# The last scan's chunks are turned by one GpSimd copy in place of two half copies

## The chip, the cores and the metric

The kernel runs on one core of a Trainium2 chip. The metric is the device time of one launch in microseconds (us), here the median of three runs. The engines of a core run side by side, each through its own instruction list, and meet at semaphores: TensorE (PE), VectorE (DVE), ScalarE (ACT), GpSimd (POOL) and SyncE (SP). A DMA is issued from the list of SP, ACT or POOL.

## The reference

```python
# L2: sums and gradients over the same edges; the gradient is what is used
def get_H(xx):
    z = xx @ W_fc.T
    e = sigmoid(concat([z[src], z[dst]]) @ W_attn.T)
    w = exp(e - segment_max(e, dst)[dst])
    h = segment_sum(w / segment_sum(w, dst)[dst] * z[src], dst)
    h1 = segment_sum((h @ W_encK.T + b_encK)[src], dst)
    K = _mlp3(h1, K_w0, ...)                      # per node
    ue = (h @ W_p1.T + b_p1)[src] + (h @ W_p2.T + b_p2)[dst]
    U = _mlp3(ue, U_w0, ...)                      # per edge
    E_new = segment_sum(K[src] * U, dst)
    return sum(E_new)
dHdx = grad(get_H)(x)
return dHdx @ J.T - dHdx @ D.T

# the whole: four layers over the same 106250 edges and 6250 nodes
x = x + L0(relu(layernorm(x)))    # graph attention
x = x + L1(relu(layernorm(x)))    # five graph convolutions with norms
x = x + L2(relu(layernorm(x)))    # the gradient above
x = x + L3(relu(layernorm(x)))    # mean over neighbours, then a product
```

In the backward pass of the third layer the gradient with respect to `ue` is one row of 64 numbers per edge, and it has to be summed twice, once over the edges with the same source and once over the edges with the same destination. The edge list is sorted by destination, so the sum over equal destinations is a running sum along the list that starts anew where the destination changes. This second sum is the stage that the change touches. The program calls it "dsum".

## The kernel before

**Layout.** 106496 edge places (106250 edges and padding) lie as 128 partitions by `J` = 832 places. A chunk is `CJ` = 32 places of each partition with 64 features, that is 128x2048 numbers of float32 (1024 KB); there are `2 * IT` = 26 chunks. In DRAM the tensor `xd` holds the 64 features of an edge side by side, and so does the buffer `DX` that a chunk is read into. A scan runs along the edges of one feature, so the chunk is first turned into feature order in a buffer `DM`: the 32 places of feature 0, then those of feature 1, and so on. `DX`, `DM`, the mask `DMASK` (in PSUM) and the output buffer `DOUT` exist twice each and alternate, chunk k uses number k % 2.

**One chunk k, in the order of its data:**

- ACT issues the read of the rows into `DX` (`rows_act`, line 2250), on its own DMA queue.
- ACT writes the mask, 0 where the destination changes (`before_scan_act`, lines 2255 and 2257).
- DVE turns features 0 to 31 (`half_turned`, line 2039) and ACT turns features 32 to 63 (line 2259). Both read `DX` in steps of 64 numbers and write `DM` without gaps. ACT's half signals `prepared`.
- DVE adds the carried sum to each feature's first place (line 624), scans twice 1024 numbers (line 629) and copies the 64 last sums into `carry` for the next chunk (line 631). This copy signals `scanned`.
- ACT turns the sums back into edge order in `DOUT` (line 2265, `dsum_out`), waits for that copy with a drain (line 2266) and issues the write to the DRAM tensor `runs` (line 2267).

**What sets the order.** Everything is written out by hand. On DVE the list per chunk is: wait for `prepared`, signal `free` (the row buffer may be filled again), the four scan instructions, then the half turn of chunk k+1. On ACT it is: issue the read of chunk k+2, output copy and write of chunk k, then mask and half turn of chunk k+2. The turns of chunk k+2 write the buffer `DM` that the output copy of chunk k reads, so they wait for `dsum_out`.

**Around the stage.** Ahead of it POOL scatters the last rows into `xd` (line 488) and DVE ends another sum. Behind it, when all 26 writes have landed, DVE signals `carried`; PE, POOL and DVE then join runs that cross partitions, and POOL fetches the 50 blocks of node sums (`ends_pool`, line 485). From its last scatter into `xd` to `carried` POOL has nothing to do.

The functions below are the five engine programs and what they call; the lines named above are the ones to look for.

Of the kernel before, what the change touches and what calls it, by code (L numbers as in the profile page):

```python
# [18 lines left out]
CJ = 32  # L19
IT = J // CJ // 2  # L20
# [58 lines left out]
def build(nc, x_in, src_in, dst_in, src_t_in, w_in, weights_in, vectors_in, out):  # L79
    ctx = ExitStack()  # L80
    with ctx:
# [8 lines left out]
        S = Semaphores()  # L90

        def sb(name, shape, dt=F32):
            return ctx.enter_context(nc.sbuf_tensor(name, shape, dt))
# [39 lines left out]
        firsts = [sb(f"first_same{b}", [P, 1]) for b in range(2)]  # L133
# [25 lines left out]
        OD, OS = Order("d", 0), Order("s", 1)  # L159
# [7 lines left out]
        def region(at, n):  # L167
            assert at + n <= SIZE
            return arena[:, at:at + n]
# [5 lines left out]
        def rows(buf, f, n=CJ):  # L175
            return buf[:, 0:n * f].rearrange("p (j f) -> p j f", f=f)
# [10 lines left out]
        def by_edge(t):  # L187
            return t[0:EP, :].rearrange("(p j) f -> p j f", j=J)
# [10 lines left out]
        def by_feature(buf, f, at=0):  # L199
            return buf[:, at * CJ:(at + f) * CJ].rearrange("p (f j) -> p f j", f=f)  # L200
# [141 lines left out]
        DX = [region(37092 + b * 2048, 2048) for b in range(2)]  # L342
        DM, DOUT = [region(41188, 2048), region(34148, 2048)], [region(19200, 2048), region(32100, 2048)]
# [19 lines left out]
        FREE = {n: TURN[n] * (IT + 1) for n in TURN}  # L363
        SCANNED = {n: TURN[n] * (2 * IT + 1) for n in TURN}
        PREPARED = {n: TURN[n] * 2 * IT for n in TURN}
        LOADS = {"scores": 16, "umlp": 32, "dsum": 16}
        LOADED = {"scores": 0, "umlp": 16 * IT, "dsum": 48 * IT}
# [6 lines left out]

        PRODUCTS = [("kvq", 32, 384), ("Wo", 32, 128), ("A", 32, 512), ("D_T", 32, 128), ("L3", 64, 64)]
        ORDINAL = {n: k for k, (n, _, _) in enumerate(PRODUCTS)}
        DEPTH = {n: d for n, d, _ in PRODUCTS}
        WIDTH = {n: w for n, _, w in PRODUCTS}

        def batches(name):  # L380
# [4 lines left out]
        for name, _, _ in PRODUCTS:  # L385
            FIRST[name] = total
            total += len(batches(name))
# [96 lines left out]
        def fetch(pool, dst, table, index):  # L484
            return pool.indirect_dma_start(dst, None, table, bass.IndirectOffsetOnAxis(ap=index, axis=0))  # L485

        def put(pool, table, index, source):
            return pool.indirect_dma_start(table, bass.IndirectOffsetOnAxis(ap=index, axis=0), source, None)  # L488
# [131 lines left out]
        def scan(dve, mask, buf, f, kept, at=0, to=None, wide=32, goes_on=None):  # L620

            to = buf if to is None else to
            first = by_feature(buf, f, at)[:, :, 0]
            dve.scalar_tensor_tensor(first, kept[:, at:at + f], m0[:] if goes_on is None else goes_on, first, ALU.mult, ALU.add)
            dve.drain()
            for a in range(0, f, wide):
                n = min(f - a, wide)
                piece = slice((at + a) * CJ, (at + a + n) * CJ)
                dve.tensor_tensor_scan(to[:, piece], mask[:, 0:n * CJ], buf[:, piece], 0.0, ALU.mult, ALU.add)  # L629
            dve.drain()  # L630
            return dve.tensor_copy(kept[:, at:at + f], by_feature(to, f, at)[:, :, CJ - 1])
# [34 lines left out]
        def ends_pool(pool, name, o, f, to):  # L666
            n = TURN[name]
            pool.wait_ge(S["carried"], n + 1)
            pool.wait_ge(S["order_joined"], o.n + 1)
            fetch(pool, joined[:, 0:f], R[f], o.join[:]).then_inc(S["join_read"], 16)  # L670
            pool.wait_ge(S["join"], n + 1)
            put(pool, R[f], o.join[:], joined[:, 0:f]).then_inc(S["joined"], 16)
            pool.wait_ge(S["joined"], 16 * (n + 1))
            for t in range(NT):
                fetch(pool, to[:, t * f:(t + 1) * f], R[f], o.end[:, t:t + 1]).then_inc(S["ends"], 16)
# [936 lines left out]
        def _(dve):  # L1612
# [346 lines left out]
            for k in range(2 * IT):  # L1959
                b = k % 2  # L1960
# [70 lines left out]

            begin(dve, carry[:, 0:64], *DMASK)

            def half_turned(k):

                dve.wait_ge(S[f"loaded{k % 2}"], LOADED["dsum"] + LOADS["dsum"] * (k // 2 + 1))
                if k >= 2:
                    dve.wait_ge(S["dsum_out"], k - 1)
                dve.tensor_copy(by_feature(DM[k % 2], 32), rows(DX[k % 2], 64).rearrange("p j f -> p f j")[:, 0:32, :])

            half_turned(0)
            for k in range(2 * IT):
                b = k % 2
                dve.wait_ge(S["prepared"], PREPARED["dsum"] + k + 1)
                dve.drain()
                dve.sem_inc(S[f"free{b}"], 1)
                scan(dve, DMASK[b], DM[b], 64, carry, goes_on=firsts[b][:]).then_inc(S["scanned"], 1)
                if k + 1 < 2 * IT:
                    half_turned(k + 1)
                dve.drain()  # L2050
            carried_dve(dve, "dsum")
            ends_dve(dve, "dsum", 64, bank[3])
# [98 lines left out]
        def _(act):  # L2151
# [77 lines left out]
            for k in range(2 * IT):  # L2229
                b = k % 2  # L2230
# [15 lines left out]

            def rows_act(k):
                b = k % 2
                act.wait_ge(S[f"free{b}"], FREE["dsum"] + k // 2 + 1)
                act.dma_start(rows(DX[b], 64), by_edge(XD)[:, step(k), :]).then_inc(S[f"loaded{b}"], 16)  # L2250

            def before_scan_act(k):
                b = k % 2
                act.wait_ge(S["scanned"], SCANNED["dsum"] + max(1, k))
                act.copy(by_feature(DMASK[b], 32)[:, :, 1:CJ],
                         OD.same[:, k * CJ + 1:(k + 1) * CJ].unsqueeze(1).broadcast_to([P, 32, CJ - 1]))
                act.copy(firsts[b][:], OD.same[:, k * CJ:k * CJ + 1])
                act.wait_ge(S[f"loaded{b}"], LOADED["dsum"] + LOADS["dsum"] * (k // 2 + 1))
                act.copy(by_feature(DM[b], 32, 32), rows(DX[b], 64).rearrange("p j f -> p f j")[:, 32:64, :]).then_inc(S["prepared"], 1)

            def after_scan_act(k):
                b = k % 2
# [6 lines left out]
            for b in range(STAGES):  # L2269
                act.wait_ge(S[f"given{b}"], 256 * len(range(b, 52, STAGES)))  # L2270
            rows_act(0)
            rows_act(1)
            before_scan_act(0)
            before_scan_act(1)
            for k in range(2 * IT):
                if k + 2 < 2 * IT:
                    rows_act(k + 2)
                after_scan_act(k)
                if k + 2 < 2 * IT:
                    before_scan_act(k + 2)  # L2280
# [173 lines left out]
        def _(pool):  # L2454
# [66 lines left out]
            def load(c):  # L2521
                if c >= STAGES:
                    pool.wait_ge(S[f"given{c % STAGES}"], 256 * (c // STAGES))
                pool.wait_ge(S[f"d_kept{c // 2 % 2}"], CREDIT + 16 * (c // 4 + 1))
                pool.dma_start(staged(c % STAGES), edges16(DE, c)).then_inc(S[f"to_give{c % STAGES}"], 16)
# [3 lines left out]
            for c in range(52):  # L2529
                pool.wait_ge(S[f"to_give{c % STAGES}"], 16 * (c // STAGES + 1))  # L2530
                for j in range(16):
                    if j == 8 and c + 2 < 52:
                        load(c + 2)
                    put(pool, XD, at_d[:, 16 * c + j:16 * c + j + 1],
                        GS[c % STAGES][:, j * 64:(j + 1) * 64]).then_inc(S[f"given{c % STAGES}"], 16)
                if c == HD_AT:
                    ends_pool(pool, "umlp", OS, P, HD)
                if c == GK_AT:
                    pool.wait_ge(S["tables_kept"], 16 * 5)
                    fetch(pool, GK[:, NS * 32:NT * 32], TB["gk"], alias_i[:]).then_inc(S["alias_whole"], 16)  # L2540
            ends_pool(pool, "dsum", OD, 64, DD)
            pool.wait_ge(S["tables_kept"], 16 * 6)
            await_made(pool, "shift_made")
# [193 lines left out]
```

## Time and profile before

| | us |
|---|---|
| median of 3 runs | 9476.88 |
| lowest and highest run | 9472.27, 9494.99 |
| the profiled execution's own time | 9485.84 |
| its span in the profile | 9484.0 |
| the stage of the change in it, first read issued to last write issued | 8170.78 to 8360.00 |
| busy over the whole span: PE, DVE, ACT, POOL | 4877.8, 4601.9, 2819.5, 5429.2 |

The engines' busy time over the whole kernel says little of one stage. The stage is read by the timeline of its stretch, by the groups of instructions in it, and by the chain that ended last, each cut to that stretch. Times inside the program are counted from the span's start.

### The profile page before, as it was taken

What the parts mean: (1) busy time and instruction counts of PE and PEld (TensorE: products, weight loads), DVE (VectorE), ACT (ScalarE), POOL (GpSimd) and SP (SyncE); (2) the same over time, 40 slices, a digit from 0 to 9 for tenths busy, and PEclk for the clock granted to TensorE, in tenths of its full rate; (3) what the DMA queues carried; (4) which work ended last, traced back from release to release, by engine and by line L of the source; (5) the groups of instructions that cost most, each with busy time, mean ns of one, the idle gap of its engine ahead of it and who ended that gap; (6) DMA issues with size and microseconds to landing.
All of it is one profiled execution on the core that took longest, in us unless ns stands there. A gap on an engine that the chain in (4) does not pass through costs nothing.

```text
span 9484.0 us, 77287 instructions
## 1 busy us (share of the span) xinstructions
PE 4877.8 (51%) x27914; PEld 2625.5 (28%) x27914; DVE 4601.9 (49%) x6100; ACT 2819.5 (30%) x2192; POOL 5429.2 (57%) x5420
## 2 busy tenths in 40 slices
PE   1000007999257777775577665344440035038976
PEld 0000006888112232331222222244430023032333
DVE  5677776777000000000298960388885510428870
ACT  0111110000000000000198950266667600429850
POOL 3777767777777777777520017688877777320000
PEclk5555555555578989887698975676765568559986
DMA  8666536443398989999799999455559948538767
GB/s 186 215 222 220 205 83 137 154 153 141 155 415 356 415 359 411 365 362 415 279 283 268 288 204 379 144 202 206 203 191 370 342 147 336 187 85 282 263 222 291
DMA packets 1203136, 2404.24 MB, mean 254 GB/s; under 512 B 566439, under 2 KB 818794, under 8 KB 1171354
## 3 DMA queue, kind: packets, MB, share of 16 engines
q1 hardware_dynamic: 996986, 2076.35, 61.7%
q0 software_dynamic: 187136, 170.29, 6.9%
q10 hardware_dynamic: 18720, 153.79, 4.2%
q8 instruction: 171, 2.80, 0.1%
q14 instruction: 123, 1.01, 0.0%
HBM read 1606.44 MB, written 711.62 MB: 244 GB/s over the span
## 4 chain that ended last, share of the span: by engine, by line
POOL 37%; DMA 25%; issue 12%; PE 11%; ACT 7%; ACTq 4%; DVE 3%; SPq 1%; DVEq 0%; POOLq 0%
POOL arena L485 18%; DMA arena<-cells_w 14%; POOL xd L488 9%; POOL cells_w L488 9%; DMA arena<-cells_c 8%; PE ps L698 6%; ACT arena L1030 3%; ACTq L1029 3%; ACT arena L1028 2%; PE ps L787 2%; PE ps L879 1%; ACTq L2266 1%; PE ps L1053 1%; PE ps L1161 1%; DMA arena<-hot 1%
## 5 line engine op out<-in xcount | busy, mean ns | idle before, releaser
L698 PE MATMUL ps<-arena 128*64 128x458 f32 (+2 forms) x7252 | 1349.0, 655 | 701.2 <-DMA arena<-cells_w 699.7
L485 POOL DMA_INDIRECT arena<-t_a,arena x832 | 945.9, 1137 | 1094.9 <-DMA t_a<-arena 841.7
L1053 PE MATMUL ps<-arena 128*33 128x400 f32 x6336 | 1165.1, 522 | 310.1 <-DVE arena L1048 302.4
L488 POOL DMA_INDIRECT sorted<-arena x832 | 839.7, 1009 | 288.9 <-issue 288.9
L716 DVE COPY carry<-ps 64x128 f32<-64x128 f32 (+1 forms) x5 | 1.5, 295 | 2048.2 <-PE ps L698 2048.2
L488 POOL DMA_INDIRECT xd<-arena x832 | 832.7, 1001 | 256.4 <-issue 253.2
L488 POOL DMA_INDIRECT cells_c<-arena x832 | 810.5, 974 | 292.6 <-issue 292.6
L488 POOL DMA_INDIRECT cells_w<-arena x832 | 813.0, 977 | 276.8 <-issue 276.8
L485 POOL DMA_INDIRECT arena<-t_kv,idx x832 | 816.9, 982 | 258.7 <-issue 253.3
L698 PEld LDWEIGHTS ps<-arena 128*64 128x64 f32 (+1 forms) x7252 | 426.2, 147 | 1621.1 <-issue 856.4
L1053 PEld LDWEIGHTS ps<-arena 128*33 128x33 f32 x6336 | 366.6, 115 | 1106.4 <-issue 652.8
L1555 ACT ACTIVATE norm_cols<-norm_cols 128x1 f32<-128x1 f32 x5 | 1.0, 203 | 2235.0 <-DVE norm_cols L1537 2235.0
L1042 DVE TENSOR_TENSOR arena<-arena 128x1600 f32<-128x1600 f32 x328 | 597.3, 1821 | 96.0 <-ACT arena L1032 42.9
L1270 PE MATMUL ps<-arena 128*128 128x50 bf16 x832 | 72.4, 219 | 1055.3 <-DVE arena L1258 1055.3
L1048 DVE SCALAR_TENSOR_TENSOR arena<-arena 128x1600 f32<-128x1600 f32 x328 | 598.8, 1826 | 25.9
L629 DVE TENSOR_TENSOR_SCAN arena<-ps,arena 128x512 f32<-128x512 f32 (+2 forms) x494 | 591.4, 1263 | 7.6
L1030 ACT ACTIVATE arena<-arena,half 128x1600 f32<-128x1600 f32 x328 | 534.5, 1630 | 24.5 <-issue 2.4
L1369 PE MATMUL ps<-arena,packT 128*128 128x50 f32 x1664 | 434.8, 412 | 0.0
L1369 PEld LDWEIGHTS ps<-arena,packT 128*128 128x128 f32 x1664 | 434.7, 336 | 0.0
L879 PE MATMUL ps<-arena 128*64 128x400 f16 x1568 | 280.9, 508 | 248.3 <-DMA arena<-cells_c 227.6
L1032 ACT ACTIVATE arena<-arena 128x1600 f32<-128x1600 f32 x246 | 374.2, 1521 | 0.0
L801 PE MATMUL ps<-ident,arena 128*64 128x128 f32 x300 | 20.7, 308 | 652.4 <-DVEq L209 651.7
(536 smaller groups left out, 9097.3 us busy)
## 6 DMA issues: line engine op xcount, KB each, us to landing
arena<-cells_w SPq DMA_DIRECT2D x245, 3200.0 KB
arena<-cells_c SPq DMA_DIRECT2D x294, 800.0 KB, 5.3
arena<-cells_turned SPq DMA_DIRECT2D x200, 800.0 KB, 8.5
cells_w<-arena SPq DMA_DIRECT2D x49, 3200.0 KB, 20.4
weighed_cells<-arena SPq DMA_DIRECT2D x68, 1600.0 KB, 14.4
arena<-weighed_cells SPq DMA_DIRECT2D x68, 1600.0 KB, 7.2
cells_c<-arena SPq DMA_DIRECT2D x50, 1600.0 KB, 5.8
cells_turned<-arena SPq DMA_DIRECT2D x100, 800.0 KB, 5.4
```

What stands on the lines that cost most here:

```text
L485: return pool.indirect_dma_start(dst, None, table, bass.IndirectOffsetOnAxis(ap=index, axis=0))
L488: return pool.indirect_dma_start(table, bass.IndirectOffsetOnAxis(ap=index, axis=0), source, None)
L629: dve.tensor_tensor_scan(to[:, piece], mask[:, 0:n * CJ], buf[:, piece], 0.0, ALU.mult, ALU.add)
L698: mm = pe.matmul(bank[base + k][g * f:(g + 1) * f, 0:m], rows_of, tile[:, g * width + at:g * width + at + m], start=first, stop=last, skip ...
L879: mm = pe.matmul(bank[(4 if i == 0 else 0) + c][64 * g:64 * g + 64, 0:400], pieces, moving[:, a:a + 400], start=first, stop=last, skip_gro ...
L1029: act.drain()
L1030: last = act.activation(expo[b], tanh[b], ACT.Exp, scale=0.5, bias=half[:])
L1032: last = act.activation(tanh[b], tanh[b], ACT.Square)
L1042: last = dve.tensor_tensor(expo[b], expo[b], piece_of(counts_of(name, p), h), ALU.mult)
L1048: dve.scalar_tensor_tensor(tanh[b], tanh[b], -1.0, expo[b], ALU.add, ALU.mult).then_inc(S["weighed"], 1)
L1053: last = pe.matmul(bank[4 * h + c][64 * kind:64 * kind + 33, 0:400], own[:, t, :], moving[:, 400 * c:400 * c + 400], start=t == 0, stop=do ...
L1369: pe.matmul(to[:, 0:NT], packT[k % 2][:, i * P:(i + 1) * P], snap[k % 2][:, i * NT:(i + 1) * NT], start=True, stop=True, skip_group_check= ...
```

## The change

POOL gets a loop over the 26 chunks ahead of `ends_pool`. For each it waits for the chunk's rows and, from the third on, for the output copy of chunk k-2, then turns all 64 features with one copy of 128x2048 and signals `dsum_turned`. DVE's and ACT's half turns go. DVE's scan of chunk k waits for `prepared` (now signalled by ACT's copy of the first mask column) and for `dsum_turned`. DVE no longer signals `free` in the loop: ACT's read of chunk k+2 waits for `dsum_turned` of chunk k.

```diff
--- before.py
+++ after.py
@@ -2031,22 +2031,11 @@
 
             begin(dve, carry[:, 0:64], *DMASK)
 
-            def half_turned(k):
-
-                dve.wait_ge(S[f"loaded{k % 2}"], LOADED["dsum"] + LOADS["dsum"] * (k // 2 + 1))
-                if k >= 2:
-                    dve.wait_ge(S["dsum_out"], k - 1)
-                dve.tensor_copy(by_feature(DM[k % 2], 32), rows(DX[k % 2], 64).rearrange("p j f -> p f j")[:, 0:32, :])
-
-            half_turned(0)
             for k in range(2 * IT):
                 b = k % 2
                 dve.wait_ge(S["prepared"], PREPARED["dsum"] + k + 1)
-                dve.drain()
-                dve.sem_inc(S[f"free{b}"], 1)
+                dve.wait_ge(S["dsum_turned"], k + 1)
                 scan(dve, DMASK[b], DM[b], 64, carry, goes_on=firsts[b][:]).then_inc(S["scanned"], 1)
-                if k + 1 < 2 * IT:
-                    half_turned(k + 1)
                 dve.drain()
             carried_dve(dve, "dsum")
             ends_dve(dve, "dsum", 64, bank[3])
@@ -2246,7 +2235,10 @@
 
             def rows_act(k):
                 b = k % 2
-                act.wait_ge(S[f"free{b}"], FREE["dsum"] + k // 2 + 1)
+                if k < 2:
+                    act.wait_ge(S[f"free{b}"], FREE["dsum"] + 1)
+                else:
+                    act.wait_ge(S["dsum_turned"], k - 1)
                 act.dma_start(rows(DX[b], 64), by_edge(XD)[:, step(k), :]).then_inc(S[f"loaded{b}"], 16)
 
             def before_scan_act(k):
@@ -2254,9 +2246,7 @@
                 act.wait_ge(S["scanned"], SCANNED["dsum"] + max(1, k))
                 act.copy(by_feature(DMASK[b], 32)[:, :, 1:CJ],
                          OD.same[:, k * CJ + 1:(k + 1) * CJ].unsqueeze(1).broadcast_to([P, 32, CJ - 1]))
-                act.copy(firsts[b][:], OD.same[:, k * CJ:k * CJ + 1])
-                act.wait_ge(S[f"loaded{b}"], LOADED["dsum"] + LOADS["dsum"] * (k // 2 + 1))
-                act.copy(by_feature(DM[b], 32, 32), rows(DX[b], 64).rearrange("p j f -> p f j")[:, 32:64, :]).then_inc(S["prepared"], 1)
+                act.copy(firsts[b][:], OD.same[:, k * CJ:k * CJ + 1]).then_inc(S["prepared"], 1)
 
             def after_scan_act(k):
                 b = k % 2
@@ -2538,6 +2528,11 @@
                 if c == GK_AT:
                     pool.wait_ge(S["tables_kept"], 16 * 5)
                     fetch(pool, GK[:, NS * 32:NT * 32], TB["gk"], alias_i[:]).then_inc(S["alias_whole"], 16)
+            for k in range(2 * IT):
+                pool.wait_ge(S[f"loaded{k % 2}"], LOADED["dsum"] + LOADS["dsum"] * (k // 2 + 1))
+                if k >= 2:
+                    pool.wait_ge(S["dsum_out"], k - 1)
+                pool.tensor_copy(by_feature(DM[k % 2], 64), rows(DX[k % 2], 64).rearrange("p j f -> p f j")).then_inc(S["dsum_turned"], 1)
             ends_pool(pool, "dsum", OD, 64, DD)
             pool.wait_ge(S["tables_kept"], 16 * 6)
             await_made(pool, "shift_made")

```

DVE's list of the stage, before: one scan and the half turn of the next chunk (the arena is the big SBUF buffer that `DX`, `DM` and `DOUT` are parts of).

```order
3356 L2039 COPY arena<-arena 128x1024 [waits loaded0]
3357 L624 SCALAR_TENSOR_TENSOR arena<-carry,first_same,arena 128x64 [waits prepared]
3358 L629 SCALAR_TENSOR_TENSOR arena<-ps,arena 128x1024 x2
3359 L631 COPY carry<-arena 128x64
3360 L2039 COPY arena<-arena 128x1024 [waits loaded1]
```

DVE's list of the stage, of the changed kernel:

```order
3356 L624 SCALAR_TENSOR_TENSOR arena<-carry,first_same,arena 128x64 [waits dsum_turned,prepared]
3357 L629 SCALAR_TENSOR_TENSOR arena<-ps,arena 128x1024 x2
3358 L631 COPY carry<-arena 128x64
3359 L624 SCALAR_TENSOR_TENSOR arena<-carry,first_same,arena 128x64 [waits dsum_turned,prepared]
3360 L629 SCALAR_TENSOR_TENSOR arena<-ps,arena 128x1024 x2
```

The copy of 128x1024 between two scans is gone, and the first instruction of a scan waits for POOL beside ACT.

ACT's list, before, from the read of chunk 2 to the read of chunk 3:

```order
1258 L2250 DMA arena<-xd 128x2048 [waits free0]
1259 L2265 COPY arena<-arena 128x2048 [waits stored0,scanned]
1260 L2267 DMA runs<-arena 128x2048
1261 L2255 CAST ps<-same_d 128x32x31 [waits scanned]
1262 L2257 CAST first_same<-same_d 128x1
1263 L2259 COPY arena<-arena 128x1024 [waits loaded0]
1264 L2250 DMA arena<-xd 128x2048 [waits free1]
```

ACT's list of the changed kernel at the same place (L2242 is the read, L2255 the output copy, L2257 the write, L2247 the mask, L2249 its first column):

```order
1256 L2242 DMA arena<-xd 128x2048 [waits dsum_turned]
1257 L2255 COPY arena<-arena 128x2048 [waits stored0,scanned]
1258 L2257 DMA runs<-arena 128x2048
1259 L2247 CAST ps<-same_d 128x32x31 [waits scanned]
1260 L2249 CAST first_same<-same_d 128x1
1261 L2242 DMA arena<-xd 128x2048 [waits dsum_turned]
```

ACT's half turn is gone, and the read waits for POOL's copy in place of DVE's signal.

POOL's list of the changed kernel behind the last scatter into `xd`; before, the row behind `L488 ... x15` was the fetch `joined<-runs,join_d`:

```order
821 L488 DMA xd<-arena 106496x64 x15
822 L2535 COPY arena<-arena 128x2048 [waits loaded0]
823 L2535 COPY arena<-arena 128x2048 [waits loaded1]
824 L2535 COPY arena<-arena 128x2048 [waits dsum_out,loaded0]
825 L2535 COPY arena<-arena 128x2048 [waits dsum_out,loaded1]
...
848 L485 DMA joined<-runs,join_d 128x64 [waits order_joined,carried]
```

26 copies stand ahead of the join fetch, two of them with no wait for an output copy.

## Rows read from the trace of the kernel before

**Rows 1.** The chain that ended last, shares by line, of 8140 to 8380 us.

```profile
by line: ACTq L2266 35.2%; ACT arena L2259 18.4%; issue 10.3%; POOL xd L488 9.3%; ACT ps L2255 4.6%; POOL arena L485 3.6%; ACTq L2267 3.3%; ACT arena L2265 3.1%; DMA arena<-xd 2.0%; DVE arena L629 1.9%; DVEq L630 1.8%; ACT first_same L2257 
```

**Rows 2.** Timeline of one steady step: start us, us, engine, line, operation, idle before.

```profile
8195.39 0.22 DVE L631 COPY carry<-arena 128x64 f32<-128x64 f32 x1
...
8196.98 3.70 ACT L2265 COPY arena<-arena 128x2048 f32<-128x2048 f32 x1
8197.22 0.35 DVE L624 SCALAR_TENSOR_TENSOR arena<-carry,first_same,arena 128x64 f32<-128x64 f32 x1 [0.66 <-ACT arena L2259]
8197.64 4.47 DVE L629 TENSOR_TENSOR_SCAN arena<-ps,arena 128x1024 f32<-128x1024 f32 x2
8200.75 0.33 ACTq L2267 DMA_DIRECT2D runs<-arena  x1
8201.11 0.99 ACT L2255 CAST ps<-same_d 128x992 f32<-128x992 bf16 x1 [0.43 <-issue]
...
8202.13 1.93 ACT L2259 COPY arena<-arena 128x1024 f32<-128x1024 f32 x1
...
8203.96 3.69 ACT L2265 COPY arena<-arena 128x2048 f32<-128x2048 f32 x1
```

**Rows 3.** Groups of instructions, 8170 to 8364 us: count | busy us, mean ns | idle before.

```profile
L2265 ACT COPY arena<-arena 128x2048 f32<-128x2048 f32 x26 | 96.1, 3696 | 4.3 <-DVE carry L631 4.3
L2259 ACT COPY arena<-arena 128x1024 f32<-128x1024 f32 x26 | 50.1, 1928 | 3.0 <-DMA arena<-xd 3.0
L2039 DVE COPY arena<-arena 128x1024 f32<-128x1024 f32 x26 | 26.8, 1032 | 113.7 <-DMA arena<-xd 113.7
L2255 ACT CAST ps<-same_d 128x992 f32<-128x992 bf16 x26 | 25.7, 989 | 631.4 <-DMA xd<-arena 620.7 <-issue 10.7
```

**Rows 4.** Timeline of the first two chunks.

```profile
8175.72 1.93 ACT L2259 COPY arena<-arena 128x1024 f32<-128x1024 f32 x1 [2.97 <-DMA arena<-xd]
...
8177.80 0.33 DVE L624 SCALAR_TENSOR_TENSOR arena<-carry,first_same,arena 128x64 f32<-128x64 f32 x1 [1.05 <-ACT arena L2259]
...
8182.77 0.21 DVE L631 COPY carry<-arena 128x64 f32<-128x64 f32 x1
...
8183.02 3.71 ACT L2265 COPY arena<-arena 128x2048 f32<-128x2048 f32 x1 [2.52 <-DVE carry L631]
8184.13 0.34 DVE L624 SCALAR_TENSOR_TENSOR arena<-carry,first_same,arena 128x64 f32<-128x64 f32 x1 [0.20 <-issue]
...
8189.08 0.22 DVE L631 COPY carry<-arena 128x64 f32<-128x64 f32 x1
```

**Rows 5.** Timeline of the last chunk.

```profile
8356.02 0.21 DVE L631 COPY carry<-arena 128x64 f32<-128x64 f32 x1
8356.27 3.66 ACT L2265 COPY arena<-arena 128x2048 f32<-128x2048 f32 x1 [1.77 <-DVE carry L631]
```

**Rows 6.** Timeline of an earlier stage, where DVE and POOL work at once.

```profile
7026.57 2.11 POOL L488 DMA_INDIRECT xd<-arena  x1 [0.31 <-issue]
7026.58 1.98 DVE L1982 COPY arena<-arena 128x2048 f32<-128x2048 f32 x1
...
7028.99 0.97 POOL L488 DMA_INDIRECT xd<-arena  x1 [0.30 <-issue]
7029.18 2.34 DVE L629 TENSOR_TENSOR_SCAN arena<-ps,arena 128x512 f32<-128x512 f32 x2
```

**Rows 7.** Line 631's copies, ns min/median/max: 5960 to 7720, then 8170 to 8364.

```profile
L631 DVE COPY carry<-arena x26: 266/324/440, 6135.9 to 7103.6; 128x128 f32<-128x128 f32 x26
...
L631 DVE COPY carry<-arena x26: 213/215/222, 8182.8 to 8356.0; 128x64 f32<-128x64 f32 x26
```

**Rows 8.** Groups of instructions on POOL: the widest and the smallest IOTA.

```profile
L2460 POOL IOTA arena<- 128x832 int32 x1 | 0.8, 811 | 0.0
...
L2458 POOL IOTA arena<- 128x1 int32 x1 | 0.1, 128 | 0.0
```

**Rows 9.** Busy us (count) per engine in 21 steady steps, PE clock, DMA share, GB/s.

```profile
8196.00:8342.00 146.00, 0.00 (x0) 0.00 (x0) 124.97 (x104) 136.62 (x84) 0.00 (x0) 0.50 0.83 299
```

## The prediction

> **What bounds the kernel now.** I read the chain of waits of the stretch first, then one step in the timeline, then the groups. In the chain, ACT's lines hold the last scan: 35.2% under the drain behind the output copy (line 2266), 18.4% under ACT's half turn (2259), 4.6% under the mask [rows 1]. DVE's scan has under 2% of it. The timeline of a step says the same: ACT goes from one output copy to the next in 8203.96 - 8196.98 = 6.98 us, and that time is its own work from end to end: 3.70 for the output copy, 4.13 from that copy's start to the mask's start (the copy, the drain and the issue of the write), 0.99 for the mask, the first column, 1.93 for its half turn. DVE waits 0.66 us for line 2259 before its scan [rows 2]. Of 146 steady microseconds ACT is busy 136.62, DVE 124.97, POOL 0; the DMA engines are at 0.83 of their time, the PE clock is 0.50 and PE has no work [rows 9]. So today the period is ACT's list, some 6.93 us: line 631 ends at 8182.98 for chunk 0 and at 8356.23 for chunk 25, 173.25 us for 25 steps [rows 4, 5].
>
> **What is removed.** ACT loses 26 half turns of 1.928 us, DVE 26 of 1.032 us, 77 us of busy time in all [rows 3]. Without them ACT needs 6.98 - 1.93 = 5.05 us a chunk. DVE needs from line 631's start to the next one's start 8189.08 - 8182.77 = 6.31 us where it hardly waits [rows 4], 5.28 without its half turn. If nothing took the place of the turns, DVE would bound the stage at about 5.3 us a chunk.
>
> **What is added.** One POOL copy of 128x2048 per chunk; call its time X. No row of the trace shows a compute copy on POOL, so I bound it. From below: POOL's widest IOTA writes 832 numbers in 811 ns and the smallest takes 128, so it writes one number in 0.82 ns and 2048 in 0.128 + 1.68 = 1.81 us, if reading cost nothing [rows 8]. But the read goes in steps of 256 bytes. ACT, with the same buffer and the same steps, has 1.928 us for 1024 and 3.696 for 2048 in its other strided copy [rows 3], or 1.73 ns a number. If the memory sets that pace for POOL too, X is 0.13 + 3.54 = 3.67 us. From above: if POOL's loop reads and then writes, the two paces add, and X is 0.13 + 3.54 + 1.68 = 5.35 us. The nearest rows are twice ACT's half turn, 3.86 us, and the output copy, 3.70; POOL's own fixed 0.13 goes on top, and I take X = 4.0 us, with 3.67 and 5.35 as likely ends and 1.81 as the far one.
>
> The Trainium skill speaks against this change: "GPSIMD Engine Reference", section "Performance pitfalls for Q7 kernels", has about 2.9 cycles for each element read with a step over 8 bytes, 1.9 for a smaller one. At its 1.2 GHz an estimate from that page is 2048 x 2.9 / 1.2 = 4.95 us, and the sum below would be +55 us with it; no run here shows such a copy yet.
>
> **Where X lies on the path.** The turn of chunk k+2 writes the buffer that the output copy of chunk k reads, so it starts only when that copy is done, as both half turns did. The loop through the buffer is: line 631 of chunk k ends, 0.04 us to ACT, 3.70 us output copy, a wake of about 0.15 (from 8177.65 to 8177.80 for ACT to DVE), X, 0.15 again, then the scan of chunk k+2 from line 624 to the end of 631, 8189.30 - 8184.13 = 5.17 us [rows 3, 4]. That loop covers two chunks, so the period is at least (9.21 + X) / 2. For X = 4.0 this is 6.6 us, a little under today's 6.93. Before, the same loop had 1.93 in the place of X and had slack, which is why ACT's list and not this loop was the bound.
>
> **A second meeting, which I think decides.** When POOL turns chunk k+2, DVE scans chunk k+1, and at the scan's end comes line 631, a copy from SBUF to SBUF. Rows 6 show such a copy and POOL excluding each other: POOL's DMA instruction started beside line 1982's copy and lasted to 7028.68, the copy ending at 7028.56, while beside the scan of line 629 (mask in PSUM) a POOL instruction took its usual 0.97 [rows 6]. Rows 7 show a cost in the other direction: line 631 takes 266 to 440 ns where POOL issues DMAs all the time, and 213 to 222 in the last scan, where POOL has nothing to do [rows 7]. So I expect line 631 to wait until POOL's copy is done. Line 624 has two SBUF inputs, but it stands before the next turn has started and should not meet one.
>
> The Trainium skill's page "SBUF — State Buffer", section "Who interferes with whom", calls this an exclusive lock on a shared port pair, held for a whole instruction. Its first half, DVE holding POOL up, is in the trace with the 2.11 us of rows 6; that a POOL copy holds DVE up for its whole length, no row here shows.
>
> With that wait, `scanned` of chunk k+1 comes after the turn of chunk k+2, and ACT's next output copy after that. The loop is now one chunk long: 0.04 + 3.70 + 0.15 + X + 0.12 + 0.21 = 4.22 + X, where 0.12 is the release seen in rows 6 and 0.21 is line 631 [rows 4, 6]. For X = 4.0 the period is 8.22 us. The turn starts 3.9 us after line 631's end and the scan wants its line 631 after 5.2, so the two meet for every X over 1.3.
>
> **The sum.** Chunks 0 to 24 are 24 periods apart, and the last step has no turn beside it: 0.18 + 5.17 = 5.35 us. That is 24 x 8.22 + 5.35 = 202.6, against 173.25: +29.4. The first scan waits for a whole turn, X, in place of ACT's 1.93 [rows 4]: +2.1. Behind the stage all stands as before; POOL's copies are all ahead of the join fetch, for which it waited anyhow. The reads of rows are issued one output copy earlier than they are used and have a period of time to land, so they stay hidden at 8.22 us; the DMA engines, at 0.83 before, are less loaded. In total +31.5 us, and in general 25 X - 68.5. The profiled execution has 9485.84 us, 9 above the median of 9476.88; the difference does not depend on it, so I add it to each: 9517 for a like execution, 9508.4 for the median. A measurement of this kernel can tell about 0.3%, 28.4 us, from no change; with the wait that is X over 3.88.
>
> **The rivals.**
>
> - *No wait at line 631.* POOL's copy and DVE's small one pass each other. For it: the only DVE copies seen beside POOL's work are delayed by 0.2 us at most, not by whole instructions [rows 7]. Against it: line 1982 did hold POOL. The period is (9.21 + X) / 2, the sum 24 times that + 5.35 - 173.25 + X - 1.93 = 13 X - 59.3. For 4.0 it is -7 us, 9469.6; for 3.67 -12; for 5.35 +10. All within 0.3%.
> - *A slow copy and the wait.* If the copy's read and write add, X = 5.35, the period is 9.57 and the sum +65, 9542. It decides how far the slower side goes.
> - *Faster: a copy at the pace of the IOTA, and no wait.* X = 1.81 gives a period of 5.5, or 5.8 if the DMAs' 0.83 x 6.97 us of work per chunk cannot shrink [rows 2, 9]: -29 to -36 us, 9441 to 9448. It needs X under 2.4 and no wait. With the wait a copy of 1.81 gives -23 us, 9454. Against it: ACT cannot read this pattern at such a pace [rows 3].
> - *The change does nothing for the busy engines.* ACT's and DVE's 77 us of busy time go in any case; in the first and second case they turn into idle time.
>
> **How the numbers follow.** The wait at line 631 gets 0.70. X over 3.88 gets 0.70 too: the nearest rows give 3.67 to 3.86 as floors, and a loop in software only adds. X under 3 gets 0.10. Both together give 0.49 for slower by over 0.3%, and 0.01 goes on top for something unseen: 0.50. Forecast and slow copy share this, 0.35 near the forecast and 0.15 far above. Faster by over 0.3% needs no wait and a fast copy: 0.03, with 0.02 for the unseen, 0.05. The rest, 0.45, is within 0.3%: no wait with any copy of 2.4 or more (about 0.28), and the wait with a copy under 3.88 (about 0.17). The range goes from the rival without the wait at X = 3.67, 9465, to the slow copy, 9542, with a microsecond or two on each side.
>
> **What would show it.** Right: POOL copies of about 4 us each starting as ACT's output copy ends; line 631 lasting or starting late until a POOL copy ends, its mean far over 215 ns or a gap ahead of it; ACT idle some 3 us per chunk ahead of the output copy; chunks 8.2 us apart. Wrong in the size: the same picture with another X, the period following it one for one. Wrong in the mechanism: line 631 still at 215 ns behind its scan while POOL's copy runs, and DVE waiting ahead of line 624 for POOL, the period following X by half. It would be wrong altogether if the reads of rows landed late, which would show as POOL waiting for `xd`.

## The result

| | median us | runs |
|---|---|---|
| kernel before | 9483.82 | 19 |
| changed kernel | 9502.77 (9487.11 to 9511.15) | 19 |
| ratio | 1.0018, 95% interval 1.0011 to 1.0025 | |

The change costs about 17 us, between 10 and 24: slower, but by less than the 0.3% that the prediction set as its bound. On another occasion the unedited changed kernel gave 1.0021 (1.0012 to 1.0030). The forecast was 9508.4 us in a range of 9463 to 9544. The mechanism that it named is in the trace; of the 31.5 us forecast, the trace has 19.9 and the medians 19.0.

Three groups of the changed kernel's last scan, of 8170 to 8390 us, answer to [rows 3] (count | busy us, mean ns | idle before). Line numbers have moved: L2255 is ACT's output copy (before L2265), L2535 the new copy on POOL. L631 is the copy of 64 sums behind each scan, with 5.6 us in all before.

```profile
L2255 ACT COPY arena<-arena 128x2048 f32<-128x2048 f32 x26 | 96.6, 3716 | 72.4 <-DVE carry L631 72.4
L2535 POOL COPY arena<-arena 128x2048 f32<-128x2048 f32 x26 | 95.0, 3656 | 106.1 <-ACT arena L2255 96.1 <-DMA arena<-xd 10.0
L631 DVE COPY carry<-arena 128x64 f32<-128x64 f32 x26 | 60.3, 2320 | 1.9
```

POOL's copy takes 3.66 us. The small copy takes 2.32 us in the mean, 0.22 before [rows 7]. ACT waits for it 72.4 us in all, where it had waited 4.3 us before [rows 3]. The timeline shows one step, and answers to [rows 2]:

```profile
8197.32 3.65 POOL L2535 COPY arena<-arena 128x2048 f32<-128x2048 f32 x1 [8.85 <-ACT arena L2255]
8197.62 0.99 ACT L2247 CAST ps<-same_d 128x992 f32<-128x992 bf16 x1 [0.43 <-issue]
...
8198.58 2.46 DVE L631 COPY carry<-arena 128x64 f32<-128x64 f32 x1
8201.07 3.73 ACT L2255 COPY arena<-arena 128x2048 f32<-128x2048 f32 x1 [2.34 <-DVE carry L631]
8201.20 0.36 DVE L624 SCALAR_TENSOR_TENSOR arena<-carry,first_same,arena 128x64 f32<-128x64 f32 x1 [0.16 <-POOL arena L2535]
8201.63 4.47 DVE L629 TENSOR_TENSOR_SCAN arena<-ps,arena 128x1024 f32<-128x1024 f32 x2
...
8204.93 3.65 POOL L2535 COPY arena<-arena 128x2048 f32<-128x2048 f32 x1 [3.96 <-ACT arena L2255]
...
8206.18 2.47 DVE L631 COPY carry<-arena 128x64 f32<-128x64 f32 x1
8208.68 3.72 ACT L2255 COPY arena<-arena 128x2048 f32<-128x2048 f32 x1 [2.34 <-DVE carry L631]
```

POOL's copy ends at 8200.97, line 631 at 8201.04, ACT starts at 8201.07. The scans themselves (line 629, 4.47 us) are untouched, with POOL's copy beside them. The period is 7.61 us: 0.03 to ACT, 3.73 the output copy, 0.13 to POOL, 3.65 the turn, 0.07 to the end of line 631. In the chain that ended last, DVE's lines have taken the place of ACT's of [rows 1]:

```profile
by line: DVE carry L631 23.2%; DVE arena L629 22.9%; DVEq L630 21.8%; POOL xd L488 10.1%; issue 6.0%; DVE arena L624 4.8%; DMA arena<-xd 1.8%; DMA runs<-arena 1.5%; POOL arena L485 1.5%; ACT arena L2255 1.4%; POOL arena L2535 1.4%; DMA join
```

The start of the stage holds one thing more (timeline; the read of the rows was issued at 8176.50):

```profile
8181.23 7.23 POOL L2535 COPY arena<-arena 128x2048 f32<-128x2048 f32 x2 [5.94 <-DMA arena<-xd]
8184.91 0.33 ACTq L2242 DMA_DIRECT2D arena<-xd  x1
8184.99 3.60 DVE L624 SCALAR_TENSOR_TENSOR arena<-carry,first_same,arena 128x64 f32<-128x64 f32 x1 [116.88 <-POOL arena L2535]
8188.67 4.47 DVE L629 TENSOR_TENSOR_SCAN arena<-ps,arena 128x1024 f32<-128x1024 f32 x2
8193.22 0.21 DVE L631 COPY carry<-arena 128x64 f32<-128x64 f32 x1
```

POOL turns the first two chunks back to back. Line 624, an operation with two inputs in SBUF, takes 3.60 us in place of 0.33 [rows 4], to the end of the second turn.

### The profile page after: what moved, and what is told of

Its sections match the earlier page's. It is cut to its first block, busy times and chain, and to the rows that moved or that the text cites. A ratio compares the mean times of both kernels' runs of the same rounds, so it can differ in the third digit from the quotient of the medians.

```text
span 9506.9 us, 77261 instructions
## 1 busy us (share of the span) xinstructions
PE 4893.7 (51%) x27914; PEld 2636.2 (28%) x27914; DVE 4641.0 (49%) x6074; ACT 2774.4 (29%) x2166; POOL 5536.2 (58%) x5446
## 4 chain that ended last, share of the span: by engine, by line
POOL 37%; DMA 25%; issue 12%; PE 11%; ACT 6%; DVE 4%; ACTq 3%; DVEq 1%; SPq 1%; POOLq 0%
POOL arena L485 18%; DMA arena<-cells_w 14%; POOL xd L488 9%; POOL cells_w L488 9%; DMA arena<-cells_c 8%; PE ps L698 5%; ACT arena L1030 4%; ACTq L1029 3%; ACT arena L1028 2%; PE ps L787 2%; DMA arena<-hot 1%; PE ps L879 1%; PE ps L1161 1%; PE ps L1053 1%; DVE carry L631 1%
## 5 line engine op out<-in xcount | busy, mean ns | idle before, releaser
L488 POOL DMA_INDIRECT sorted<-arena x832 | 844.2, 1015 | 289.6 <-issue 289.6
L488 POOL DMA_INDIRECT xd<-arena x832 | 835.2, 1004 | 256.5 <-issue 253.5
L488 POOL DMA_INDIRECT cells_c<-arena x832 | 813.2, 977 | 293.1 <-issue 293.1
L488 POOL DMA_INDIRECT cells_w<-arena x832 | 815.9, 981 | 275.9 <-issue 275.9
L1270 PE MATMUL ps<-arena 128*128 128x50 bf16 x832 | 72.4, 219 | 1057.0 <-DVE arena L1258 1057.0
```

## The experiments

The theory: a copy on POOL and a DVE operation that uses a second way into SBUF (a copy from SBUF to SBUF, or an operation with two inputs there) exclude each other; so line 631 waits, and through it ACT. The rivals: the loop through the two buffers `DM` holds the stage up; POOL's copy is simply too long, whatever it meets; the reads of the rows come late.

The stage is compared by the time from the start of the first line 631 to the start of the last, 25 steps: 173.2 us before (8182.8 to 8356.0, [rows 7]), 188.4 in the changed kernel (8193.2 to 8381.6).

The first four kernels shared a chip on which the earlier stages took about 4000 us longer (the kernel before 13606.67 us, with 13234.67 to 13935.94 between runs). Of them only the last scan's rows are used. One of the four is the kernel before with its carry moved, and it has before's own period there (173.3 us for 25 steps), which shows that these rows can be used.

**Carry in PSUM, twice.** The 64 carried sums move out of SBUF. Line 631 then writes PSUM, line 624 has one SBUF input.

```diff
-            begin(dve, carry[:, 0:64], *DMASK)
+            dcarry = bank[7][:, 0:64]
+            begin(dve, dcarry, *DMASK)
...
-                scan(dve, DMASK[b], DM[b], 64, carry, goes_on=firsts[b][:]).then_inc(S["scanned"], 1)
+                scan(dve, DMASK[b], DM[b], 64, dcarry, goes_on=firsts[b][:]).then_inc(S["scanned"], 1)
...
+            dve.tensor_copy(carry[:, 0:64], dcarry)
+            dve.drain()
             carried_dve(dve, "dsum")
```

> The changed kernel with the 64 carried sums kept in PSUM during the last scan (copied to SBUF once at its end), so that the small copy behind each scan (line 631) writes PSUM and the first operation of a scan (line 624) has one SBUF tensor input. If the small copy waits because it and GpSimd's copy exclude each other, it takes about 0.2 us again, ScalarE's output copy follows it at once, and the period falls from 7.61 us to the two-chunk loop, (9.2 + 3.66) / 2 = 6.4 us: 24 x 1.2 = 28 us less than the changed kernel, and the first scan does not wait for the second turn, 3 us more. Against the kernel before that is about -13 us, ratio 0.9987. If DVE is held up by something else (a semaphore, GpSimd slowing all of VectorE), the period stays at 7.6.

> The changed kernel with the carried sums in PSUM, once more, because its first run shared a chip whose times varied by 700 us. Its last scan was 168.2 us long there (first small copy to last), against 188 of the changed kernel and 173 of the kernel before, with GpSimd waiting for the rows in most chunks. By that the kernel should be about 20 us under the changed kernel plus 3 us for the first scan, and 3 to 5 us under the kernel before: ratio 0.9994 to 0.9999.

Measured: in both runs line 631 takes 0.27 to 0.30 us with POOL's copy around it. The timeline of the second run (L2538 is POOL's copy, L2258 the output copy, L2245 the read of rows, L2260 the write):

```profile
8252.79 3.67 POOL L2538 COPY arena<-arena 128x2048 f32<-128x2048 f32 x1 [2.31 <-DMA arena<-xd]
8252.92 0.99 ACT L2250 CAST ps<-same_d 128x992 f32<-128x992 bf16 x1 [0.43 <-issue]
8252.96 0.40 ACTq L2245 DMA_DIRECT2D arena<-xd  x1
8253.84 0.19 ACT L2252 CAST first_same<-same_d 128x1 f32<-128x1 bf16 x1
8255.53 0.27 DVE L631 COPY ps<-arena 128x64 f32<-128x64 f32 x1
8255.83 3.68 ACT L2258 COPY arena<-arena 128x2048 f32<-128x2048 f32 x1 [1.81 <-DVE ps L631]
...
8259.88 3.70 POOL L2538 COPY arena<-arena 128x2048 f32<-128x2048 f32 x1 [3.42 <-DMA arena<-xd]
```

The group of POOL's copies in the same run:

```profile
L2538 POOL COPY arena<-arena 128x2048 f32<-128x2048 f32 x26 | 95.6, 3681 | 81.5 <-DMA arena<-xd 71.1 <-ACT arena L2258 10.4
```

Line 631 runs inside POOL's copy (8252.79 to 8256.46) and ACT follows at once. The 25 steps take 168.2 and 167.4 us, some 20 less than in the changed kernel, and the kernel is back at the time before: 0.9996 (0.9987 to 1.0005). Line 624 had 328 ns in the mean, with no long one among the 26, so its wait in the first chunk is gone as well. This settles the main question: POOL's copy is as long as before (3.68 us), so its length alone was not the cause. It also narrows what waits. In its first chunk line 624, now with one of its two tensor inputs in PSUM, took 0.33 us inside POOL's second turn, and the scans, with their mask in PSUM, took their usual time. Both read and write SBUF as well, so reading and writing SBUF once beside POOL's copy is not by itself enough for a wait. What passed had one tensor operand in PSUM, what waited had none; which of the small copy's two ends in SBUF held it, no run separates.

It misses the 6.4 us period expected: it is 6.7, and POOL waits for its rows 71.1 us in all (in the timeline the read was issued at 8252.96, and the copy of those rows started at 8259.88). ACT issued that read behind its output copy and write, though POOL's copy of 8246.81 had freed the row buffer at 8250.48. That the reads behind ACT's list are the next bound is what these waits suggest; no run changed them alone in this kernel.

**Carry in PSUM in the kernel before**, as the control.

> Control: the kernel before with the carried sums in PSUM in the same way. GpSimd has nothing to do in that stage and ScalarE's list sets the period, so both theories expect no difference: period 6.93 to 6.98 us, the kernel's time within 3 us of the kernel before.

Measured: line 631 from 12417.0 to 12590.3 us, 173.3 for 25 steps. No difference, as both theories said; moving the carry gains nothing by itself, only against POOL's copy.

**Three buffers in feature order.**

```diff
-        DM, DOUT = [region(41188, 2048), region(34148, 2048)], ...
+        DM, DOUT = [region(41188, 2048), region(34148, 2048), region(12800, 2048)], ...
...
-                if k >= 2:
-                    pool.wait_ge(S["dsum_out"], k - 1)
+                if k == 2:
+                    pool.wait_ge(S["scanned"], SCANNED["dsum"] + 1)
+                if k >= 3:
+                    pool.wait_ge(S["dsum_out"], k - 2)
```

with `DM[k % 3]` in POOL's copy, the scan and the output copy.

> The changed kernel with three buffers in feature order in place of two, so that the turn of chunk k+2 waits for the output copy of chunk k-1 and not of chunk k. The carry stays in SBUF. If the buffer were what holds the changed kernel up, the period would fall to about 5.4 to 5.8 us. If the wait of the small copy is what holds it up, a turn still lies beside the end of some scan: the small copy still waits, and the period stays between 6.6 us (the turn started by the landing of its rows) and 7.6 us (started by the output copy).

Measured: 11945.0 to 12121.7 us, 176.7 for 25 steps, 7.07 a step; between the two bounds of the exclusion theory. Two neighbouring steps say more than the mean (L2537 is POOL's copy):

```profile
12003.45 3.65 POOL L2537 COPY arena<-arena 128x2048 f32<-128x2048 f32 x1 [2.22 <-DMA arena<-xd]
12006.28 0.89 DVE L631 COPY carry<-arena 128x64 f32<-128x64 f32 x1
...
12008.35 3.79 POOL L2537 COPY arena<-arena 128x2048 f32<-128x2048 f32 x1 [1.24 <-DMA arena<-xd]
...
12012.30 0.21 DVE L631 COPY carry<-arena 128x64 f32<-128x64 f32 x1
```

The first POOL copy ends at 12007.10, and line 631, begun at 12006.28, at 12007.17. The second ends at 12012.14, and line 631, begun 0.16 later, takes its 0.21. The longest small copy of this run starts just behind a POOL copy and lasts as long as it does:

```profile
12038.66 3.63 POOL L2537 COPY arena<-arena 128x2048 f32<-128x2048 f32 x1 [5.11 <-DMA arena<-xd]
12038.74 3.62 DVE L631 COPY carry<-arena 128x64 f32<-128x64 f32 x1
```

All 26 follow this: 17 overlap a POOL copy and end 0.06 to 0.14 us behind it, the other 9 take 0.21 to 0.22.

**Three buffers, the rows read by SyncE.** In the run above the start of a turn was mostly set by its rows. Here SP issues the reads, as soon as a row buffer is free.

```diff
+            for k in range(2 * IT):
+                b = k % 2
+                if k < 2:
+                    sp.wait_ge(S[f"free{b}"], FREE["dsum"] + 1)
+                else:
+                    sp.wait_ge(S["dsum_turned"], k - 1)
+                sp.dma_start(rows(DX[b], 64), by_edge(XD)[:, k * CJ:(k + 1) * CJ, :]).then_inc(S[f"loaded{b}"], 16)
```

in SP's list behind `back_sp(sp, range(2))` and the waits for `given`, and no `rows_act` in ACT's.

> The changed kernel with three buffers in feature order and the reads of the rows issued by SyncE as soon as their row buffer is free, where ScalarE's list delayed them in the run with three buffers. The carry stays in SBUF. Nothing but the output copy of chunk k-1 then holds a turn back, and it ends 3.9 us after a small copy, in the middle of the next scan: by the exclusion theory the small copy of that scan waits and the period is again near 4.0 + 3.66 = 7.6 us. If the buffers or the late reads were the cause, the period falls to about 5.8 us, what the DMA engines need for 2 MB a chunk.

Measured: ratio 1.0019 (1.0009 to 1.0028), line 631 from 8198.4 to 8383.6 us, 185.2 for 25 steps, with 2210 ns in the mean:

```profile
L2525 POOL COPY arena<-arena 128x2048 f32<-128x2048 f32 x26 | 94.7, 3643 | 98.1 <-ACT arena L2247 90.7 <-DMA arena<-xd 7.4
L631 DVE COPY carry<-arena 128x64 f32<-128x64 f32 x26 | 57.5, 2210 | 1.9
```

With more buffers and early rows the step is back at 7.4 us in the mean, against 7.5 in the changed kernel: nearly all of POOL's idle time ends with an output copy (90.7 us), in the middle of the next scan. The loop through the buffers is excluded as the cause, and so are the rows.

**The same with the carry in PSUM.**

> The same with the carried sums in PSUM, so that no VectorE operation of the loop excludes GpSimd's copy. ScalarE needs 5.05 us a chunk, VectorE 5.4, GpSimd 3.7, the DMA engines 5.7 to 5.8 (0.83 of 6.97 us before). Period about 5.8 us, 145 us for 25 steps in place of 173 before and 188 in the changed kernel: 26 us less than the kernel before, ratio 0.997.

Measured: ratio 0.9980 (0.9971 to 0.9989), 9458.85 us against 9478.74 for the kernel before and 9499.40 for the changed kernel on the same chip. It beats both, the kernel before by 0.2%. It differs from the run above in the carry alone. 25 steps take 152.6 us (8176.6 to 8329.2), 6.1 each; one of the shorter ones in the timeline (L2528 is POOL's copy, L2250 the output copy, L2252 the write):

```profile
8262.64 0.27 DVE L631 COPY ps<-arena 128x64 f32<-128x64 f32 x1
8262.70 0.19 ACT L2244 CAST first_same<-same_d 128x1 f32<-128x1 bf16 x1
8262.95 3.79 ACT L2250 COPY arena<-arena 128x2048 f32<-128x2048 f32 x1
8263.07 0.35 DVE L624 SCALAR_TENSOR_TENSOR arena<-ps,first_same,arena 128x64 f32<-128x64 f32 x1 [0.16 <-ACT first_same L2244]
8263.50 4.47 DVE L629 TENSOR_TENSOR_SCAN arena<-ps,arena 128x1024 f32<-128x1024 f32 x2
8266.80 0.33 ACTq L2252 DMA_DIRECT2D runs<-arena  x1
8266.87 3.80 POOL L2528 COPY arena<-arena 128x2048 f32<-128x2048 f32 x1 [1.66 <-ACT arena L2250]
8267.17 0.99 ACT L2242 CAST ps<-same_d 128x992 f32<-128x992 bf16 x1 [0.43 <-issue]
8268.04 0.27 DVE L631 COPY ps<-arena 128x64 f32<-128x64 f32 x1
```

5.4 us lie between these two small copies. Other steps take longer, for a reason that the waits name (engine and line, for whom: us in total, times, longest):

```profile
POOL arena L2528 <- ACT arena L2250: 38.4, 16, 4.8
POOL arena L2528 <- DMA arena<-xd: 23.7, 9, 6.0
DVE arena L624 <- ACT first_same L2244: 21.6, 24, 4.1
ACT arena L2250 <- DMA runs<-arena: 19.7, 8, 4.2
```

ACT waits 19.7 us for its earlier writes to `runs` to land, which it did nowhere before. Over 8200 to 8325 us the DMA engines are busier than in the kernel before (same columns as [rows 9]; before first, then this run):

```profile
8200.00:8325.00 125.00, 0.00 (x0) 0.00 (x0) 106.72 (x90) 116.92 (x73) 0.00 (x0) 0.50 0.83 299
8200.00:8325.00 125.00, 0.00 (x0) 0.00 (x0) 101.99 (x81) 97.42 (x61) 72.68 (x20) 0.50 0.89 329
```

That the transfers are the next bound fits, but no run here took bytes away to show it. The expectation of 5.8 us was 0.3 too low.

**A copy that turns nothing.** POOL copies the same 128x2048 numbers, reading them without gaps; the turning is left out.

```diff
-                pool.tensor_copy(by_feature(DM[k % 2], 64), rows(DX[k % 2], 64).rearrange("p j f -> p f j"))...
+                pool.tensor_copy(by_feature(DM[k % 2], 64), by_feature(DX[k % 2], 64))...
```

> The changed kernel with GpSimd's copy of the same 128x2048 numbers reading without gaps, so nothing is turned (the turning is left out). If the step of 256 bytes sets the copy's pace, it takes about 1.8 to 2.1 us in place of 3.66, and since the period follows it one for one it comes to about 5.9 us: 24 x 1.7 = 41 us less than the changed kernel. If the copy's loop on GpSimd sets the pace, it stays near 3.7 us and the time stays.

Measured (group of POOL's copies):

```profile
L2535 POOL COPY arena<-arena 128x2048 f32<-128x2048 f32 x26 | 49.2, 1893 | 299.8 <-DMA arena<-xd 270.1 <-ACT arena L2255 29.7
```

1.893 us against 3.656: the step of 256 bytes costs POOL 1.76 us, nearly half of its copy. The 25 steps took 157.2 us (12430.6 to 12587.8), 6.3 each and not the 5.9 expected, and POOL waited for rows ahead of 19 of 26 copies; as above, that points to the reads behind ACT's list. Line 631 still waited, 0.57 us in the mean, where the shorter copy reached the end of a scan.

**Half of the change.** GpSimd takes ACT's features 32 to 63, DVE keeps features 0 to 31.

```diff
-                act.copy(by_feature(DM[b], 32, 32), rows(DX[b], 64).rearrange("p j f -> p f j")[:, 32:64, :]).then_inc(S["prepared"], 1)
...
+                pool.tensor_copy(by_feature(DM[b], 32, 32), rows(DX[b], 64).rearrange("p j f -> p f j")[:, 32:64, :]).then_inc(S["dsum_turned"], 1)
```

> One part of the change alone: GpSimd takes over ScalarE's half of the turning (features 32 to 63), VectorE keeps its own. Half a copy takes 0.1 + 1.8 = 1.9 us on GpSimd. ScalarE's list falls from 6.97 to about 5.05 us, VectorE's stays at 6.31 and becomes the bound. The half copy starts 3.9 us after the small copy's end and lasts until 5.8; the small copy wants to run at 5.2, so it waits some 0.5 us. By the exclusion theory the period is 6.3 to 6.6 us, 159 us or a little more for 25 steps, 13 us less than the kernel before (ratio 0.9986); without exclusion it is 6.3. Either way it should beat both kernels.

> GpSimd turns features 32 to 63 only, VectorE the others, and the carried sums are in PSUM. In the run without PSUM the small copy took 0.43 us in the mean in place of 0.21, and 25 steps 165.5 us. With PSUM it takes 0.27 whatever GpSimd does. If that wait was all, the steps shrink by 0.2 us, to about 161 us; if GpSimd's late start (it waited for the rows in most chunks) sets the period, nothing changes.

Measured: without PSUM the ratio is 0.9995 (0.9986 to 1.0004), 25 steps in 165.5 us (8175.0 to 8340.5), against 159 expected; with PSUM 0.9989 (0.9980 to 0.9998), 163.4 us (8177.8 to 8341.2), against 161. The groups of the first of the two:

```profile
L2545 POOL COPY arena<-arena 128x1024 f32<-128x1024 f32 x26 | 51.0, 1962 | 124.0 <-DMA arena<-xd 111.2 <-ACT arena L2264 12.8
...
L631 DVE COPY carry<-arena 128x64 f32<-128x64 f32 x26 | 11.1, 426 | 1.9
```

The half copy costs the 1.9 us foreseen. The expectation put the small copy 5.2 us behind the one before it and left out DVE's half turn between them; it comes 6.2 us behind (8247.66 to 8253.82 in the trace), when a half copy started by the output copy would have been over. But POOL starts most of them when the rows land, some 0.8 us later, and so they meet.

The 6.5 us above 159 can be read from the same trace. The step from the small copy at 8174.98 to the one at 8181.36 meets no POOL copy and takes 6.38 us, 159.5 for 25; line 631 takes 5.5 us more over the scan than before (11.1 against 5.6). Together that is 165.0 of the 165.5. DVE's list is the bound, and 159 was this list without the wait. PSUM for the carry takes that wait away but gains only 2.1 us, as the groups of that run show:

```profile
L2040 DVE COPY arena<-arena 128x1024 f32<-128x1024 f32 x26 | 29.1, 1118 | 116.9 <-DMA arena<-xd 116.8 <-issue 0.2
L631 DVE COPY ps<-arena 128x64 f32<-128x64 f32 x26 | 7.3, 281 | 1.9
```

DVE's own half turn (line 2040) has both ends in SBUF too and takes 2.2 us more than before (26.8 in [rows 3]), and the small copy into PSUM 1.7 more.

**The changed kernel again.**

> The changed kernel once more, unedited, on the same chip as the three others, since the first four experiments ran on a chip whose earlier stages took some 4000 us longer. Its last scan should read as in its first profile: GpSimd's copy 3.66 us, the small copy behind a scan 2.3 us in the mean, a period of 7.61 us, about 188 us from the first small copy to the last.

Measured: ratio 1.0021 (1.0012 to 1.0030), line 631 from 8182.9 to 8370.7 us, 187.8, with 2303 ns; POOL's copy 3640 ns.

## Why the prediction was right, and what was off

- **What bound the stage before**: right. The trace before is the evidence: ACT went from one output copy to the next without waiting for another engine. The runs agree: with the half turns off ACT and the wait at line 631 gone, 25 steps fell from 173.2 us to 167.4 with two buffers and to 152.6 with three and early rows, while moving the carry alone left 173.3.
- **The wait at line 631** (0.70): right, and it decided. Three kernels show it from three sides: gone with PSUM, present in one step and absent in the next with three buffers, back in full with early rows. [rows 6] had shown one direction only; the trace after shows the other, for a whole instruction. My use of [rows 7] for it was weak: the slower small copies there, 266 to 440 ns, have 128 columns and the faster ones 64, so only the spread above 266, at most 0.17 us, can come from POOL. The Trainium skill's "SBUF — State Buffer", section "Who interferes with whom", calls it an exclusive lock for the whole instruction; the runs agree, with 2.46 us for a copy of 0.22 in the steady steps, and 3.62 where the small copy started just behind POOL's.
- **X**: 3.66 us, not 4.0. My low end, 0.13 + 3.54 = 3.67 from ACT's pace for the same steps and POOL's smallest IOTA, was the value. That the two agree so closely may be chance: no run shows that one thing sets the pace of both engines. The push upwards for a loop in software was not needed. At 25 us for each microsecond of X it made 8.6 us of the error. The estimate of 4.95 us from the Trainium skill's "GPSIMD Engine Reference", section "Performance pitfalls for Q7 kernels", does not agree with the 3.66 us of this trace; the measurement decides.
- **The release**: I put 0.12 for it and 0.21 for line 631 behind POOL's copy. Both together took 0.07. All 24 small copies that met POOL's ended 0.06 to 0.08 us behind it, less than the 0.21 that one takes alone; what the copy does while it waits no run shows. That is 0.26 us a step, 6.2 in 24.
- **Line 624 in the first chunk**: missed. I wrote that it should not meet a turn, and did not look at the first two turns, which run back to back. It cost 3.25 us. The steady steps are as I said.
- **The sum**: 31.5 - 8.6 - 6.2 + 3.3 = 20.0. The trace has 188.4 - 173.2 = 15.2 for the steps and 16.9 - 12.2 = 4.7 from the first read's issue to the end of the first line 631, 19.9 in all. The profiled span grew by 22.9; 5.7 of that had come before the first read was issued, which the change does not touch, and some of it went again behind the stage. The medians differ by 18.95.
- **The range and the chances**: the time lies in the range. By the bound of 0.3% the result is "same" (0.45) and not "slower" (0.50): I had named X over 3.88 as the turning point, and gave it 0.70 where rows put it just under. That 9502.77 lies only 5.6 us from the forecast is in part luck: the change cost 12.6 us less than forecast by the medians, and the kernel before measured 6.9 us more in the 19 runs than in the three that the forecast started from.
- **The rival without the wait** would have had a period of 6.4 us by its formula. The run that makes it real had 6.7: the statement that the reads stay hidden held for the long period only.

## What to carry to other kernels

Before work goes to GpSimd's idle time, list what VectorE runs beside it. Beside GpSimd's copies here, a float32 copy within SBUF or an operation with two SBUF inputs waited until the GpSimd copy was over, even with 64 columns, and whoever waited for that operation waited too. If it is a short one on a loop of dependencies, put its output or one input into PSUM; here that one edit was worth as much as the change had cost. To price a strided copy for an engine without a row of its own, another engine's row with the same step came close in this one case (3.70 us on ACT, 3.66 on POOL).

## What the runs showed of the hardware

- The scan with its mask in PSUM is not disturbed by POOL's copy: 2277 ns in the mean in the changed kernel, 2278 before ([rows 2] has 4.47 us for two).
- A copy on POOL writes and reads 2048 numbers per partition in 1.89 us without gaps and 3.66 with steps of 256 bytes, 0.92 and 1.79 ns each; ACT has 1.80 for the latter [rows 3].
- With the carry in PSUM the small copy took 0.27 to 0.30 us, 0.21 to 0.22 with both ends in SBUF and nothing beside it.
- It goes both ways. In the half kernel with PSUM the first POOL copy, started just behind a DVE copy, took 2.76 us, where the median of the 26 is 1.93:

```profile
8169.73 1.03 DVE L2040 COPY arena<-arena 128x1024 f32<-128x1024 f32 x1 [116.75 <-DMA arena<-xd]
8169.76 2.76 POOL L2548 COPY arena<-arena 128x1024 f32<-128x1024 f32 x1 [6.12 <-DMA arena<-xd]
```
